# Output tile in two buffers, its block transpose moved later; the scaled key-key and key-query copies each one VectorE product

## The reference, cut to what matters

```python
mixed = silu(causal_conv1d(hidden @ w_qkv, conv_w))          # 4 taps
q, k, v = split(mixed)                                       # 16 key heads, 32 value heads, 128 wide
q, k = l2norm(q), l2norm(k)
for t in range(512):                                         # per batch and value head
    St = St * exp(g_t)
    delta = (v_t - k_t @ St) * b_t
    St = St + outer(k_t, delta)
    o_t = q_t @ St
core = o * rsqrt(mean(o * o) + eps) * norm_weight * silu(hidden @ w_z)
x = x + core @ w_out
```

## Time and profile before

| | before |
|---|---|
| median of 3 runs | 3383.51 us (3382.04 to 3384.68) |
| the profiled execution, its own time | 3382.74 us |
| its span | 3380.9 us |
| granted TensorE clock, mean | 0.99 |
| busy: PE, DVE, ACT, POOL | 3202.4 us (95%), 2222.3 (66%), 1794.1 (53%), 1946.0 (58%) |
| `store_o` (L586): DMAs, median from issue to landing | 1024, 1.7 us |

### The profile page before, as it was taken

One profiled execution on the slowest core, in us unless ns is written; L12 is line 12 of the kernel. 1 busy time (PEld: TensorE's weight loads), 2 busy tenths in 40 slices (PEclk: granted clock), 3 DMA queues, 4 the chain that ended last, 5 costly groups with the idle time before them and its releaser, 6 DMA issues. The chain is left out here.

```text
span 3380.9 us, 59978 instructions
## 1 busy us (share of the span) xinstructions
PE 3202.4 (95%) x20064; PEld 2087.9 (62%) x20064; DVE 2222.3 (66%) x3366; ACT 1794.1 (53%) x5623; POOL 1946.0 (58%) x1888
## 2 busy tenths in 40 slices
PE   5899999999999999999999999999988999999999
PEld 2567666766676667666766666666663444454444
DVE  6788888878888888888888887888840100024553
ACT  2466666666666666666666666666652000011232
POOL 2677777777777777777777777777740000011132
PEclk8999999999999999999999999999989999999999
DMA  3233333333333333333343333333325222211001
GB/s 100 58 91 92 92 85 86 92 87 86 80 101 89 86 84 95 90 80 85 91 98 87 80 90 93 89 80 92 101 70 196 75 100 87 99 38 63 0 13 38
DMA packets 469200, 282.30 MB, mean 83 GB/s; under 512 B 311808, under 2 KB 410240, under 8 KB 463360
## 3 DMA queue, kind: packets, MB, share of 16 engines
q1 hardware_dynamic: 467600, 271.39, 30.2%
q10 hardware_dynamic: 1296, 7.09, 0.5%
HBM read 173.17 MB, written 88.34 MB: 77 GB/s over the span
## 5 line engine op out<-in xcount | busy, mean ns | idle before, releaser
L762 PE MATMUL acc<-xT,wc 128*128 128x512 f32 x2048 | 937.0, 601 | 9.4 <-ACT d_kks L1230 7.4
L762 PEld LDWEIGHTS acc<-xT,wc 128*128 128x128 f32 x2048 | 370.8, 191 | 381.2 <-issue 380.7
L1019 DVE SCALAR_TENSOR_TENSOR d_conv<-acc,wc,d_conv 128x511 f32<-128x511 f32 (+2 forms) x768 | 566.2, 737 | 36.6 <-ACT d_conv L1182 25.2
L775 PE MATMUL acc<-wc,xT 128*128 128x256 f32 x2048 | 473.4, 384 | 0.0
L775 PEld LDWEIGHTS acc<-wc,xT 128*128 128x128 f32 x2048 | 379.1, 190 | 46.3
L1064 DVE CAST_PREDICATED d_zm<-cons,d_tz 128x512 f16<-128x512 int32 x384 | 265.4, 691 | 160.3 <-PE d_tz L807 153.6
L1057 DVE STREAM_TRANSPOSE d_em<-d_dm 128x1024 f16<-128x1024 f16 x256 | 314.8, 1230 | 40.8 <-ACT d_dm L1246 40.8
L1542 PE MATMUL acc<-t_area 128*128 128x512 f32 x768 | 332.5, 592 | 0.8 <-ACT t_area L1991 0.8
L2048 POOL TENSOR_SCALAR t_veps<-t_mv 128x1 f32<-128x1 f32 x32 | 9.7, 303 | 546.1 <-DVE t_mv L1787 546.1
L1246 ACT ACTIVATE d_dm<-acc 128x512 f16<-128x512 f32 x384 | 229.8, 598 | 121.8 <-PE acc L820 121.8
L1182 ACT ACTIVATE d_conv<-acc,wc 128x512 f32<-128x512 f32 x256 | 177.2, 692 | 219.8 <-PE acc L762 172.0
(11 more groups left out here) (224 smaller groups left out, 6979.2 us busy)
## 6 DMA issues: line engine op xcount, KB each, us to landing
d_decay<-decay_rows SPq DMA_DIRECT2D x64, 512.0 KB, 5.1
v_rows<-d_vb SPq DMA_DIRECT2D x256, 128.0 KB, 2.6
d_vn<-v_rows SPq DMA_DIRECT2D x64, 512.0 KB, 3.7
core_rows<-d_ob SPq DMA_DIRECT2D x1024, 32.0 KB, 1.7
t_area<-core_rows SPq DMA_DIRECT2D x30, 1024.0 KB, 4.8
wc<-in_w SPq DMA_DIRECT2D x96, 256.0 KB, 3.1
k_rows<-d_kf SPq DMA_DIRECT2D x256, 64.0 KB, 3.2
d_kn<-k_rows SPq DMA_DIRECT2D x64, 256.0 KB, 2.9
```

The lines of the kernel that those rows point to most:

```text
L762: last = nc.tensor.matmul(bank(TILE[j])[:, :], wtile(j, k), xT[:, k, r % B * S:(r % B + 1) * S], start=k == 0, stop=k == KT - 1)
L775: last = nc.tensor.matmul(bank(f"z{j}")[:, i * GV * P:(i + 1) * GV * P].rearrange("p (h n) -> p h n", h=GV), xT[:, k, r % B * S + (2 * j + ...
L1019: nc.vector.scalar_tensor_tensor(c[:, d:S], bank(TILE[j])[:, 0:S - d], tap(j, KS - 1 - d), c[:, d:S], ALU.mult, ALU.add).then_inc(taps, 1)
```

## The change

`oo` becomes two tiles, used in turn by iterations. `flip_o` moves on DVE from behind `level_z(m, 2)` to behind `flip_d(m, 3)`. The two copies leave ACT and become one DVE product each: `copy_kq` stands where `flip_o` stood, `copy_kk` behind `next_state(s, 1, *)`. `junk` shrinks; k's squares are written over `kf`, and six of the eight output squares over `ob`, once the DMAs that read it have landed. `flip_k` waits for the squares of k in place of the store.

```diff
-        oo = sb("oo", [P, GV, NC, P])
-        junk, kqs, kks = sb("junk", [P, 3 * NC, P], BF16), sb("kqs", [P, S]), sb("kks", [P, S])
+        oo = many("oo", 2, [P, GV, NC, P])
+        junk, kqs, kks = sb("junk", [P, GV, P], BF16), sb("kqs", [P, S]), sb("kks", [P, S])
...
             def flip_k(n):
                 dve.wait_ge(silued, nth(n, "silued", 0))
-                wait(dve, k_moved, at(back(n, 1), 80, 64))
+                wait(dve, k_squares, at(back(n, 1), NC, NC))
...
+            def copy_kk(n):
+                dve.wait_ge(kk_done, count(n))
+                dve.wait_ge(rk_ready, at(n, 3, 2))
+                wait(dve, bf_ready, at(back(n, 1), GV, GV))
+                nc.vector.tensor_tensor(by_chunk(kks), by_chunk(bank("kk")), per_token(rk[n[1] % 2][:, 0, :]), ALU.mult).then_inc(kk_copied, 1)
...
                 if invert:
                     flip_d(m, 1)
                     level_z(m, 2)
-                if finish:
-                    flip_o(f)
+                    copy_kq(m)
...
                 if recur:
                     next_state(s, 1, 0)
                     next_state(s, 1, 1)
+                if project:
+                    copy_kk(n)
...
                 if invert:
                     level_z(m, 4)
                     flip_d(m, 3)
+                if finish:
+                    flip_o(f)
...
             def first_output(s):
                 act.wait_ge(o_done, at(s, NC, 1))
-                wait(act, o_flipped, count(s, 1))
+                wait(act, o_flipped, count(s, 2))
...
+                if (c, h) in ((1, 0), (0, 1)):
+                    out = junk[:, h, :]
+                else:
+                    wait(act, stored, at(back(s, 1), STORES, STORES))
+                    out = ob[:, c, h * NC:(h + 1) * NC, :].rearrange("p b j -> p (b j)")
...
                 if project:
                     k_square(n)
-                if invert:
-                    copy_kq(m)
                 if recur:
                     first_output(s)
...
-                if project:
-                    copy_kk(n)
                 if invert:
                     copy_d(m, 3)
```

More of the change, by code:

```diff
@@ L441, in delta_rule @@
                       "z0": (z_silued, "z_silued", 0), "z1": (z_silued, "z_silued", 1),
-                      "kk": (kk_copied, "squares", NC - 1), "kq": (kqs_ready, "squares", NC - 1)}
+                      "kk": (kk_copied, "once", 0), "kq": (kqs_ready, "once", 0)}
         CONV_ORDER = ("k", "v1", "v0", "q")
@@ L612, in k_norm @@
                 pool.wait_ge(rk_ready, at(n, 3, 1))
-                wait(pool, kqs_ready, at(back(n, 2), NC, NC))
+                wait(pool, kqs_ready, count(n, 2))
                 wait(pool, v_scaled, at(back(n, 2), NC, NC))
@@ L655, in b_full @@
             def b_full(n, h):
-                pool.wait_ge(kk_copied, at(n, NC, NC))
+                pool.wait_ge(kk_copied, count(n))
                 pool.wait_ge(gams_ready, nth(n, "gams_ready", h))
@@ L661, in p_full @@
             def p_full(m, h):
-                pool.wait_ge(kqs_ready, at(m, NC, NC))
+                pool.wait_ge(kqs_ready, count(m))
                 pool.wait_ge(gamc_ready, nth(m, "gamc_ready", h))
@@ L691, in o_gate @@
             def o_gate(s, h):
-                o = oo[:, h, :, :]
+                o = oo[s[1] % 2][:, h, :, :]
                 pool.wait_ge(o_scaled, at(s, GV * NC, h * NC + NC))
@@ L1048, in flip_o @@
                 wait(dve, stored, at(back(s, 1), STORES, STORES))
-                nc.vector.transpose(ob[:, :, :, :], oo[:, :, :, :].rearrange("p h c (a j) -> p a (h c) j", a=NC)).then_inc(o_flipped, 1)
+                dve.wait_ge(o_squares, at(s, GV * NC, GV * NC))
+                nc.vector.transpose(ob[:, :, :, :], oo[s[1] % 2][:, :, :, :].rearrange("p h c (a j) -> p a (h c) j", a=NC)).then_inc(o_flipped, 1)
             def flip_e0(m):
@@ L1085, in next_state, with copy_kq @@
                                                chunk(psa, h), ALU.mult, ALU.add).then_inc(s_ready, 1)
+            def copy_kk(n):
[3 more added lines that the diff above has]
+                nc.vector.tensor_tensor(by_chunk(kks), by_chunk(bank("kk")), per_token(rk[n[1] % 2][:, 0, :]), ALU.mult).then_inc(kk_copied, 1)
+            def copy_kq(m):
+                dve.wait_ge(kq_done, count(m))
+                dve.wait_ge(rk_ready, at(m, 3, 2))
+                wait(dve, p_ready, at(back(m, 1), GV, GV))
+                nc.vector.tensor_tensor(by_chunk(kqs), by_chunk(bank("kq")), per_token(rk[m[1] % 2][:, 0, :]), ALU.mult).then_inc(kqs_ready, 1)
             def output(s, c):
@@ L1089, in output @@
                 dve.wait_ge(oq_ready, at(s, 6, 2 * c))
-                nc.vector.tensor_tensor(oo[:, :, c, :], psb[:, 0:GV * P].rearrange("p (h d) -> p h d", h=GV),
+                nc.vector.tensor_tensor(oo[s[1] % 2][:, :, c, :], psb[:, 0:GV * P].rearrange("p (h d) -> p h d", h=GV),
                                         oq[:, :].rearrange("p (h d) -> p h d", h=GV), ALU.add).then_inc(o_ready, 1)
@@ L1206, in k_square @@
                 wait(act, k_squares, at(back(n, 1), NC, NC))
-                squares(lambda c: kn[n[1] % 2][:, :, c, :], lambda c: junk[:, c, :].rearrange("p (a j) -> p a j", j=32), kss, k_squares)
+                squares(lambda c: kn[n[1] % 2][:, :, c, :], lambda c: kf[:, :, c, :], kss, k_squares)
             def q_square(n):
@@ L1223, in b_high @@
                 nc.scalar.activation(bh[n[1] % 2][h][:, :], bf[h][:, :], ACT.Copy).then_inc(bh_ready, 1)
[L1225 to L1230, removed]
             def o_scale(s, h):
@@ L1234, in o_scale @@
                 for c in range(NC):
-                    o = oo[:, h, c, :]
+                    o = oo[s[1] % 2][:, h, c, :]
                     nc.scalar.activation(o, o, ACT.Copy, scale=r2[:, h, c:c + 1]).then_inc(o_scaled, 1)
[L1238 to L1242, removed]
             def copy_d(m, l):
@@ L1271, in first_output @@
                 act.wait_ge(o_done, at(s, NC, 1))
-                wait(act, o_flipped, count(s, 1))
-                nc.scalar.activation(oo[:, :, 0, :], psb[:, 0:GV * P].rearrange("p (h d) -> p h d", h=GV), ACT.Copy).then_inc(first_ready, 1)
+                wait(act, o_flipped, count(s, 2))
+                nc.scalar.activation(oo[s[1] % 2][:, :, 0, :], psb[:, 0:GV * P].rearrange("p (h d) -> p h d", h=GV), ACT.Copy).then_inc(first_ready, 1)
             def o_square(s, c, h):
@@ L1280, in o_square @@
                     act.wait_ge(o_ready, at(s, NC - 1, c))
-                nc.scalar.activation(junk[:, NC + h * NC + c, :], oo[:, h, c, :], ACT.Square, scale=HD ** -0.5,
+                if (c, h) in ((1, 0), (0, 1)):
[3 more added lines that the diff above has]
+                    out = ob[:, c, h * NC:(h + 1) * NC, :].rearrange("p b j -> p (b j)")
+                nc.scalar.activation(out, oo[s[1] % 2][:, h, c, :], ACT.Square, scale=HD ** -0.5,
                                      accum_out=oss[:, h, c:c + 1]).then_inc(o_squares, 1)
```

## The result

| | before | after |
|---|---|---|
| median | 3384.1 us (3382.04 to 3386.13, 4 runs) | 3453.92 us (3444.88 to 3460.03, 4 runs) |
| ratio | | 1.0204, 95% interval 1.018 to 1.0228 |
| the profiled execution, its own time and span | 3382.74, 3380.9 us | 3444.88, 3443.1 us |
| granted TensorE clock, mean | 0.99 | 0.980 |
| busy: PE, DVE, ACT | 3202.4, 2222.3, 1794.1 us | 3236.4, 2300.1, 1666.4 us |

The change made the kernel 2% slower. The forecast was 3388 us, within 3355 to 3445; the measured time lies 9 us above the upper end.

What follows compares the result with a forecast made beforehand. The prediction took PE as the bound, busy 482.5 of 500 us. Its terms, -93 saved, +64 for late taps, +11 and +22 for late kn, sum to +4 us: 3388 us, range 3355 to 3445.

Steps and rivals of the forecast that it cites:

- saved by the two waits: PE's waits for d_rr (residual) and d_dm (copy_d) go: 1.5 us a slot, 62 slots, 93 us saved.
- taps late in a group's first slot: Convolution tap weights, issued on SP behind the late store, come 4.3 us later in 15 first slots: 64 us.
- kn late, all other slots: kn reaches ACT's squares of k late: 11 us in 31 plain slots, 22 in 16 last slots of groups.
- the first wait: PE's wait for DVE's d_rr ahead of solve (L881), 0.97 us a slot, was to go.
- the second: PE's wait for ACT's d_dm ahead of d_tz, 0.61 us a slot, was to go except for about 0.1.
- A: Start of a slot, at PE's d_tz product; flip_o was to end at A + 3.6 instead of A - 5.1.
- My limit of A + 30.9: Latest arrival of kn at no cost to PE; in plain slots it was put at A + 30.8.
- The products: The two new DVE products, copy_kq and copy_kk: 0.65 us each, in DVE's idle time, costing nothing.
- The loop through SP closes in every slot: Rival: the loop from flip_o through SP and kn back to flip_o has no slack; 3445 us, chance 0.22.
- SP is not late: Rival: only the DVE lateness of the taps is left, 21 us; 3312 us, half way 3350, chance 0.12.
- DVE the second bound: Rival: copy_kk frees its bank 0.5 us late in each slot, 31 us; 3419 us, chance 0.10.
- the waits stay: Rival: copy_d of level 3 finds another late instruction ahead, 0.61 us in 62 slots unsaved; 3426 us, chance 0.05.

Runs made afterwards that it cites:

- flip_early: The changed kernel with flip_o directly behind residual(s, 1, *), ahead of flip_d(m, 2): 3299.04 us, ratio 0.9753.
- early_act: flip_early with copy_kk and copy_kq back on ACT in four pieces each: 3321.05 us, ratio 0.9811.
- late_taps: flip_early with SP's output store also waiting for DVE's last flip of the slot, only ahead of a new group's tap weights: 3379.73 us, ratio 0.999.
- fill_taps: late_taps with the eight level_e(s, 5) products on PE issued 18 times in a group's first slot: 3372.28 us, ratio 0.9958.
- store_late: flip_early with SP's store_o also waiting for DVE's level 3 transpose, flip_d(m, 3): 3397.82 us, ratio 1.0043.

## Why the prediction was wrong

The sum was -93 + 64 + 11 + 22 = +4 us for the profiled execution; its span grew by 62.2. Term by term, the saving being flip_early's span (3297.1) less that of before:

| term | forecast | measured |
|---|---|---|
| saved by the two waits | -93 | -83.8 |
| taps late in a group's first slot | +64 | +61.7 |
| kn late, all other slots | +33 | +40.6 |
| PE's longer busy time, nearly all slow clock | none | +40.7 |
| sum | +4 | +59.2, and 3 us of other idle time |

**The step that failed** is the sum itself: it prices a stall by its length, at full clock on both sides. For the taps it says "So each group's first slot grows by 4.3: 64 us", and no term stands for what the matmuls behind it cost. PE's busy time is 40.7 us above that of flip_early, which has the same matmuls, and 34.0 above the kernel before, whose short waits lengthen its own busy time as in early_act. flip_early, late_taps and fill_taps show the cause: no gap, full clock; gaps of 2.4 to 4.2 us, 25.5 us lost; gaps filled with work, 4 us lost. Without the 40.7 the time would have been about 3413, inside the range. No row of before had such a stall in its steady part, and the profile's 1.00 there was taken for a property of the kernel and not of its lack of gaps. The prediction has no rival for it either.

**The saving** was 9 us too high: not 1.5 a slot but 84 / 62 = 1.35. Comparing PE's steps between starts over all slots, flip_early against before, the two waits gave more than forecast, 62.1 and 41.9 us, 104 for 93. But PE, which is now earlier, takes longer at two other steps: 15.6 us from the level products to `read_k` (L860) and 5.6 from kk's products (L782) to the level product behind them. No term stood for these 21 us; what holds PE there was not tested. That each half, run apart, came out about as I had put it (64 for 0.97 x 62 = 60, and 37 for 0.51 x 62 = 32) is luck: by steps early_act's gain is the first wait, 63, and over half of the second, 23, less the 21 and some smaller ones.

**The taps** were right: 15 waits of 4.1 us against 4.3, with `flip_o` at A + 3.57 against A + 3.6.

**kn** was 8 us too low in all. The 14 waits of groups' last slots have 23.3 us (22 forecast), and the 18 of the other slots 17.3 (11 forecast). I had put the wait at A; in the trace it comes at `read_q` (L868), which needs ACT's first output, queued behind the squares of k. My limit of A + 30.9 looked at the wrong reader. How much of the 7.6 us is due to that and how much to scatter of the issue times was not measured.

**The median** stands 9.0 above the profiled execution here, not 0.8. The other executions list a mean clock of 0.975 to 0.977, against 0.980: they spent more time at low clock. That makes 66 us in all: 40.7 longer busy time, 9.2 saving, 7.6 kn, 8.2 median, 3 other idle time, less 2.3 for the taps.

**The products** took 0.68 us each, inside the bounds of 0.6 to 0.75, the first row for kk and the second for kq (count, then shortest, median and longest in ns):

```profile
L1092 DVE TENSOR_TENSOR d_kks<-acc,d_rk x64: 676/683/692, 89.7 to 2525.6; 128x512 f32<-128x512 f32 x64
...
L1098 DVE TENSOR_TENSOR d_kqs<-acc,d_rk x64: 674/676/684, 115.3 to 2553.2; 128x512 f32<-128x512 f32 x64
```

Only one wait of PE for the bank that `copy_kk` frees is listed in the whole run, 7.2 us, at the start, where the kernel before has one of 7.4. They cost nothing that shows, as argued. Nor do the squares that go over `ob`: flip_early has them too, and there ACT waits for a store's landing once, 2.1 us.

**The rivals.** "The loop through SP closes in every slot" gave 3445, near the measured time for another reason: PE waits in 18 of the plain slots and not all, and kn costs 7.6 us more than forecast in all, where that rival wants 57. That it came within 9 us of the time is luck. "SP is not late" fell by the SP rows. "DVE the second bound" fell by flip_early, and "the waits stay" by PE's waits.

## What to carry to other kernels

When an instruction that releases a DMA is moved, walk the whole queue of the engine that issues it up to the first transfer that someone waits for; here the same transposition, ten instructions earlier or later on an engine that had room for both, was the difference between 0.975 and 1.020. When that walk ends in a stall of PE that was not there before, add what the matmuls behind it take at half the clock. For each us of stall PE's busy time grew here by 0.4 us in the changed kernel, 0.5 in late_taps and 0.6 in store_late. If an edit has a good half and a bad half, as the double buffer and the late place had here, look for the place that keeps the first alone before giving up both.

## What the runs showed of the hardware

- PE's granted clock fell from 2.4 to 1.2 GHz behind a single gap in an otherwise full stream. Over the 13 traces, between 150 and 2400 us, such a stretch began inside or within 4 us behind 61 of 61 gaps above 2.8 us, 16 of 23 from 2.4 to 2.8, 28 of 43 from 1.8 to 2.4, and 7 of 54 from 1.0 to 1.8. In late_taps this made each us of waiting cost 1.5 us (25.5 more for 50.2).
- In fill_taps, where the gap was filled with 4.0 us of 64-column f16 products (0.23 us for eight), the granted clock stayed at 1.00. The Trainium skill, TensorE: Matmul & The Clock Gate, section "HAM oscillation — how this bites in real kernels", describes a kernel that waits for a DMA in each round, finds its clock low at each start and pays for it each time. The changed kernel's trace agrees: in each of 15 groups PE waits behind a late DMA, 3.5 us at 1142 us, with 0.50 granted behind it.
- SP needs 0.49 us (7.89 for 16) for each DMA of the output store in the slot shown, and 0.67 (10.64 for 16) for each q move. With 16 each in a slot of 37 us, half of SP's time is issuing them. A later start moves what stands behind it by less than its own lateness as long as SP had been waiting in between: the store of that slot starts at A + 3.6, and in a plain slot of the kernel before (A = 1175.00) at A - 5.0, 8.6 later; the q moves start at A + 11.6 for A + 5.1, 6.5 later, since SP had waited 2.4 us ahead of them.
